# Tap rows of a deformable convolution: the multiply and the adds move from VectorE to GpSimd

## The chip, the cores and the metric

One Trainium2 chip, one core of it. The kernel is a hand-scheduled program: each engine has its own list of instructions, and semaphores hold them together. The metric is the device time of one execution in microseconds (us); of the kernel before there are three timed runs and one profiled execution. Engine names in the profile: PE is TensorE, DVE is VectorE, ACT is ScalarE, POOL is GpSimd, SP is SyncE (it only issues DMAs here).

## What is computed

A batch of 16 images of 128 channels and 56x56 pixels goes through four residual layers, each on the group-normalised image. The change sits in the second, a deformable convolution:

```python
xproj = inp @ in_w + in_b
x1 = gelu(layernorm(depthwise_conv(x)))
offset = x1 @ off_w + off_b                       # 16 groups x 9 points x (x, y)
mask = softmax((x1 @ mask_w + mask_b).reshape(N, H, W, G, P), -1)
out = _dcnv3_core(xproj, offset, mask)            # bilinear samples around each pixel, weighted by mask
out = out @ out_w + out_b
...
x = x + _L0_conv_ref(_gn(x), ...)   # whitening of 8 groups of channels
x = x + _L1_conv_ref(_gn(x), ...)   # the deformable convolution above
x = x + _L2_conv_ref(_gn(x), ...)   # attention in 7x7 windows, then between windows
x = x + _L3_conv_ref(_gn(x), ...)   # 3x3 convolution of a masked image
```

Where all offsets are below one pixel, a sample reads only the 3x3 pixels around its grid point, so the nine points together read a 5x5 neighbourhood. The bilinear weight of a point is a product of two "hats" (functions of the offset in x and in y, three values each), and the whole layer is a convolution with 25 taps whose weights differ from pixel to pixel.

## The kernel before

Samples are pipelined: one turn of the main loop (15 turns) holds the window attention of sample i beside the first steps of sample i+1 (the *windows* stretch, 32 steps `s`), and then the deformable convolution of sample i+1 beside the last two layers of sample i (the *tile* stretch). Sample 0's tile stretch stands alone ahead of the loop. The tile stretch is `sample_tiles`: 7 tiles `c` (112 partitions, each 4 pixels wide), and 5 steps `dy` in each. On every engine the program's order is what is written there; no engine may run ahead of a semaphore.

For tile `c` the steps are these.

- PE projects offsets and mask logits, ACT copies them (L1231) and makes the hats in two halves (`hats`, L1239 to L1245, at dy 1 and 2 of tile c-1). `hats` first waits for the count 3c of `k_s`, that is, until all tap rows of tile c-1 are built, since both tiles use one hat buffer.
- DVE takes the softmax of the mask: `shift_mask` (L1658, L1659) at dy 1 of tile c-1, then, after ACT's exponential, `sum_mask` and `norm_mask` (L1665 to L1671) and `rows_by_mask` (L1678), which multiplies the y hats by the mask, all at dy 3 of tile c-1.
- DVE builds the tap rows in `by_row(n, c, bb)`, bb = 0, 1, 2: one product of 1728 elements (L1690) and three additions of 576 elements into the tap weights `kw` (L1696), each waiting for the one before. bb 0 runs at dy 4 of tile c-1, bb 1 and 2 after the multiplies of dy 0 and 1 of tile c. The last addition of each raises `k_s`. For tile 0 they run in the last steps of the windows stretch and after the first multiply.
- DVE's `multiply(n, c, dy)` (L1713) makes 25 x 512 products of taps and pixels in five instructions of 2560 elements. For dy 0, 1, 2 it waits for `k_s` of bb 0, 1, 2. PE adds them up with identity matmuls (`sum_taps`, L888 and L890); the product ring holds two, so a multiply also waits for the sum two turns before.
- POOL only clears: the tap weights `kw` of each tile (L552, L556), the image, and a few paddings.

Behind each half step stands one item of the last two layers (`after_windows(i, q)`): reading the windows back from HBM, the attention between windows (q 2 to 19), the aggregation and projection (q 20 to 36; PE L978 and L988, ACT L1321, DVE L1909), the mask of the last layer (DVE L1922 to L1953) and its 63 groups of convolution matmuls (L689). SP's queue waits for `k_s` 3 of tile 0 before it loads 2 MB of weights (`load_wqk2`), and the tokens of the windows (which DVE reads at L1878, q 2) are loaded behind that in the same queue.

Below, E(c) is the moment at which the tap rows of tile c are complete (the end of the last of its three groups at L1696), and M(c) the end of `rows_by_mask` of tile c (L1678).

Of the kernel before, what the change touches and what calls it, by code (L numbers as in the profile page):

```python
# [28 lines left out]
PT = TY * TX  # L29
# [30 lines left out]
DVE_PRE, DVE_MAIN, DVE_BLK, DVE_END = 6 + 8 * DW_BLOCKS, 105, 69, 46  # L60
# [53 lines left out]
def build(nc, a):  # L114
    with ExitStack() as ctx:
# [180 lines left out]
        t_main = sem("act_own_main")  # L296
# [74 lines left out]
        def alone(eng):  # L371
            eng.sem_inc(s_passed, 1)
# [159 lines left out]
        def _(pool):  # L532
# [14 lines left out]
            def zero_taps(i, n):  # L547
                for u in range(2):
                    if i is not None:
                        pool.wait_ge(s_p.sem, s_p.at(i, PAIRS if u else PAIRS - 4))  # L550
                        alone(pool)
                    nc.gpsimd.memset(kw[u][0:PT, :], 0.0).then_inc(k_z.sem, 1)  # L552
                for c in range(2, TR):
                    pool.wait_ge(pr_s.sem, pr_s.at(n, (c - 1) * SHIFTS))
                    alone(pool)
                    nc.gpsimd.memset(kw[c % 2][0:PT, :], 0.0).then_inc(k_z.sem, 1)  # L556

# [15 lines left out]
            zero_taps(None, 0)  # L573
            with pool.Fori(0, N - 1) as i:
                zero_windows(i)
                zero_taps(i, i + 1)
# [813 lines left out]
        def _(dve):  # L1390
# [283 lines left out]
            def rows_by_mask(n, c):  # L1674
                logits, hat = logits_of(c), offsets_of(c)[1]
                dve.wait_ge(ht_s.sem, ht_s.at(n, 2 * c + 2))
                ownm.settle()
                ownm.mark(V.tensor_tensor(hat[0:PT, :, 1, :], hat[0:PT, :, 1, :],  # L1678
                                          logits.rearrange("p (a n) -> p a n", a=1).to_broadcast([PT, 3, HN]),
                                          ALU.mult))  # L1680

            def by_row(n, c, bb):

                tt, hat = terms if c else om_first, offsets_of(c)[1]
                if bb:
                    dve.wait_ge(k_s.sem, k_s.at(n, 3 * c + bb))
                else:
                    ownm.settle()
                    dve.sem_inc(rw_s.sem, 1)
                ownm.step(V.tensor_tensor(tt[0:PT, :].rearrange("p (a n) -> p a n", a=3), hat[0:PT, :, 0, :],  # L1690
                                          hat[0:PT, bb, 1:2, :].to_broadcast([PT, 3, HN]), ALU.mult))
                if bb == 0:
                    dve.wait_ge(k_z.sem, k_z.at(n, c + 1))
                for aa in range(3):
                    k5 = kw[c % 2][0:PT, :].rearrange("p (y x n) -> p x y n", y=5, x=5)[:, aa:aa + 3, bb:bb + 3, :]
                    ins = V.tensor_tensor(k5, k5, tt[0:PT, aa * HN:(aa + 1) * HN].rearrange(  # L1696
                        "p (x y n) -> p x y n", x=3, y=3), ALU.add)
                    if aa == 2:
                        ins.then_inc(k_s.sem, 1)
                    else:  # L1700
                        ownm.step(ins)
# [77 lines left out]
            def before_last(s, n):  # L1779
# [12 lines left out]
                elif s == OFF_AT + 4:  # L1792
                    rows_by_mask(n, 0)
                elif OFF_AT + 5 <= s < OFF_AT + 7:
                    by_row(n, 0, s - (OFF_AT + 5))
# [164 lines left out]
            def sample_tiles(n, i):  # L1960
                dve.wait_ge(cp_img.sem, cp_img.at(n))
                alone(dve)
                for c in range(TR):
                    ahead = c + 1 < TR
                    for dy in range(SHIFTS):
                        s = c * SHIFTS + dy
                        multiply(n, c, dy)
                        if dy == 0:
                            by_row(n, c, 1 if c else 2)
                        elif c and dy == 1:  # L1970
                            by_row(n, c, 2)
# [17 lines left out]
                        elif ahead and dy == 4:  # L1989
                            by_row(n, c + 1, 0)  # L1990
# [79 lines left out]
```

## Time and profile before

| | us |
|---|---|
| three timed runs: lowest, median, highest | 10003.76, 10026.43, 10063.13 |
| the profiled execution, its own time | 10047.3 |
| its span | 10045.3 |
| mean granted TensorE clock | 0.897 of full speed |
| busy: PE, DVE, ACT, POOL | 8162.0, 7406.0, 3949.2, 191.2 |

The profiled execution is 0.2% above the median of the timed runs. The profile gives each engine's busy time, the chain that ended last, groups of instructions by line with the idle time ahead of them and what ended it, and a timeline. A turn of the loop lasts about 588 us; the turn looked at below has its tile stretch from about 3465 to 3785 us of the span.

### The profile page before, as it was taken

What the parts mean: (1) busy time and instruction counts of PE and PEld (TensorE: products, weight loads), DVE (VectorE), ACT (ScalarE), POOL (GpSimd) and SP (SyncE); (2) the same over time, 40 slices, a digit from 0 to 9 for tenths busy, and PEclk for the clock granted to TensorE, in tenths of its full rate; (3) what the DMA queues carried; (4) which work ended last, traced back from release to release, by engine and by line L of the source; (5) the groups of instructions that cost most, each with busy time, mean ns of one, the idle gap of its engine ahead of it and who ended that gap; (6) DMA issues with size and microseconds to landing.
All of it is one profiled execution on the core that took longest, in us unless ns stands there. A gap on an engine that the chain in (4) does not pass through costs nothing.

```text
span 10045.3 us, 287502 instructions
## 1 busy us (share of the span) xinstructions
PE 8162.0 (81%) x123582; PEld 4563.3 (45%) x123582; DVE 7406.0 (74%) x8864; ACT 3949.2 (39%) x6124; POOL 191.2 (2%) x253
## 2 busy tenths in 40 slices
PE   6468888887988888798888879888887888888796
PEld 5324445353544535354453534445353444545354
DVE  2488777878777786877778687777868777786863
ACT  0034434253443435334353533434353343535332
POOL 0000000000000000000000000000000000000000
PEclk7579998998989899898999989898998989999898
DMA  4001101111110111111011111101111110111101
GB/s 113 6 13 35 49 20 46 37 38 40 42 44 22 46 31 45 41 37 48 24 46 31 45 41 33 53 22 46 31 45 42 30 54 24 46 31 45 41 25 52
DMA packets 230299, 391.48 MB, mean 39 GB/s; under 512 B 25200, under 2 KB 166480, under 8 KB 221776
## 3 DMA queue, kind: packets, MB, share of 16 engines
q1 hardware_dynamic: 229008, 372.66, 13.3%
q8 instruction: 1006, 16.48, 0.7%
q14 instruction: 285, 2.33, 0.1%
HBM read 192.47 MB, written 130.55 MB: 32 GB/s over the span
## 4 chain that ended last, share of the span: by engine, by line
PE 59%; DVE 22%; issue 11%; ACT 6%; DMA 1%; DVEq 1%; SPq 0%; POOL 0%; ACTq 0%; POOLq 0%
PE ps L888 10%; PE ps L689 7%; PE ps L753 7%; DVE arena L1713 4%; PE ps L786 4%; PE ps L988 4%; PE ps L802 4%; PE ps L761 3%; PE ps L978 3%; DVE arena L1768 3%; PE ps L710 3%; PE ps L775 2%; DVE arena L1690 2%; DVE arena L1696 2%; PE ps L922 1%
## 5 line engine op out<-in xcount | busy, mean ns | idle before, releaser
L888 PE MATMUL ps<-arena,ident 64*64 64x512 f32 x5600 | 1739.1, 677 | 745.8 <-DVE arena L1713 745.6
L890 PE MATMUL ps<-arena,ident 48*64 48x512 f32 x5600 | 1742.6, 678 | 0.0
L1713 DVE TENSOR_TENSOR arena<-arena 112x2560 f32<-112x2560 f32 x560 | 1578.2, 2819 | 100.5 <-PE ps L890 93.6
L888 PEld LDWEIGHTS ps<-arena,ident 64*64 64x64 f32 x5600 | 488.6, 148 | 1775.6 <-issue 1764.0
L753 PE MATMUL ps<-arena,wqk 128*128 128x400 f32 x2048 | 909.6, 564 | 152.6 <-DVE arena L1817 119.6
L689 PE MATMUL ps<-vp,convw 128*128 128x448 f32 x2016 | 821.3, 549 | 23.6 <-ACT vp L1310 23.6
L1696 DVE TENSOR_TENSOR arena<-arena 112x576 f32<-112x576 f32 x1008 | 764.2, 758 | 34.9
L802 PE MATMUL ps<-arena 64*64 64x33 f32 x32768 | 656.0, 229 | 127.0 <-issue 71.1
L1808 DVE TENSOR_REDUCE arena<-ps 128x16 f32<-128x800 f32 x512 | 504.9, 986 | 294.9 <-PE ps L775 290.6
L1802 DVE COPY arena<-ps 128x400 f32<-128x400 f32 x512 | 293.0, 572 | 568.2 <-PE ps L753 568.0
L1231 ACT ACTIVATE arena<-ps 112x864 f32<-112x864 f32 x224 | 199.2, 889 | 1299.8 <-PE ps L710 1295.1
L802 PEld LDWEIGHTS ps<-arena 64*64 64x64 f32 x32768 | 586.0, 144 | 229.2 <-issue 228.2
L786 PE MATMUL ps<-ident,arena 128*128 128x128 f32 x4096 | 577.4, 286 | 132.3 <-ACT arena L1109 43.8
L1690 DVE TENSOR_TENSOR arena<-arena 112x1728 f32<-112x1728 f32 x336 | 655.3, 1950 | 0.2 <-DVE arena L1678 0.2
L761 PE MATMUL ps<-wv,arena 128*64 128x256 f32 x4096 | 600.1, 417 | 37.7 <-ACT arena L1179 37.2
L753 PEld LDWEIGHTS ps<-arena,wqk 128*128 128x128 f32 x2048 | 336.1, 198 | 621.1 <-ACT arena L1166 205.9
L1173 ACT ACTIVATE arena<-arena 128x800 f32<-128x800 f32 x512 | 447.1, 873 | 367.4 <-DVE arena L1810 364.2
L689 PEld LDWEIGHTS ps<-vp,convw 128*128 128x128 f32 x2016 | 364.9, 189 | 456.2 <-issue 432.5
L775 PEld LDWEIGHTS ps<-arena 32*64 32x64 f32 x32768 | 400.0, 134 | 332.0 <-issue 324.1
L786 PEld LDWEIGHTS ps<-ident,arena 128*128 128x128 f32 x4096 | 457.1, 145 | 178.9 <-issue 128.5
L1179 ACT ACTIVATE arena<-ps 128x512 f32<-128x512 f32 x512 | 305.5, 597 | 586.7 <-PE ps L786 586.4
L1768 DVE SCALAR_TENSOR_TENSOR arena<-vp,cols,arena 128x896 f32<-128x896 f32 (+1 forms) x512 | 525.3, 1026 | 1.0
(299 smaller groups left out, 12542.5 us busy)
## 6 DMA issues: line engine op xcount, KB each, us to landing
windows_out<-arena SPq DMA_DIRECT2D x1024, 100.0 KB
arena<-windows_out SPq DMA_DIRECT2D x224, 256.0 KB, 4.2
arena<-windows_out SPq DMA_DIRECT2D x224, 192.0 KB, 3.4
arena<-in_wqk SPq DMA_DIRECT2D x16, 2048.0 KB, 8.5
arena<-in_x_t SPq DMA_DIRECT2D x16, 1568.0 KB, 10.5
arena<-in_x SPq DMA_DIRECT2D x16, 1568.0 KB, 7.3
arena<-arena SPq DMA_DIRECT2D x32, 784.0 KB
out_x<-xb SPq DMA_DIRECT2D x112, 224.0 KB, 2.0
```

The source lines that it names most:

```text
L689: mm = nc.tensor.matmul(ps[:, bank, 0:CH], weights[:, tap, :], vp[:, ROWS * k + dy:ROWS * k + dy + ROWS, dx:dx + W], start=(tap == 0), sto ...
L753: nc.tensor.matmul(ps[:, 5 - m % 2, 0:NWY * NTOK], wqk[:, m * C:(m + 1) * C], xwb[b % 2][:, :, 0:NTOK], start=True, stop=True).then_inc(qk ...
L761: mm = nc.tensor.matmul(ps[hh * SLOT:(hh + 1) * SLOT, 4, wi * 256:(wi + 1) * 256], xwb[b % 2][:, 2 * pr + wi, :], wv[:, hh * 256:(hh + 1) ...
L775: mm = nc.tensor.matmul(ps[wi * SLOT:(wi + 1) * SLOT, r, place * NTOK:(place + 1) * NTOK], qk[b % 2][32 * r:32 * r + 32, m, w:w + SLOT], q ...
L786: mm = nc.tensor.transpose(ps[:, 4 + q, k * C:(k + 1) * C], e_sb[u][:, 8 * q + 2 * k:8 * q + 2 * k + 2, :], ident)
L802: mm = nc.tensor.matmul(ps[wi * SLOT:(wi + 1) * SLOT, 6 + hh, (kk * 4 + r) * VD:(kk * 4 + r + 1) * VD], et[u][hh * SLOT:(hh + 1) * SLOT, a ...
L888: nc.tensor.matmul(ps[half, 3, :], ident[0:SLOT, 0:SLOT], prod[0:SLOT, ring(c, dy), dx, :], start=(s < 2), stop=(s >= TAPS - 2), skip_grou ...
L890: mm = nc.tensor.matmul(ps[half, 4, :], ident[SLOT:PT, SLOT:], prod[SLOT:PT, ring(c, dy), dx, :], start=(s < 2), stop=(s >= TAPS - 2), ski ...
L1690: ownm.step(V.tensor_tensor(tt[0:PT, :].rearrange("p (a n) -> p a n", a=3), hat[0:PT, :, 0, :], hat[0:PT, bb, 1:2, :].to_broadcast([PT, 3, ...
L1696: ins = V.tensor_tensor(k5, k5, tt[0:PT, aa * HN:(aa + 1) * HN].rearrange("p (x y n) -> p x y n", x=3, y=3), ALU.add)
L1713: V.tensor_tensor(prod[0:PT, ring(c, dy), :, :].rearrange("p k (n e) -> p k n e", e=CG), taps.to_broadcast([PT, SHIFTS, N64, CG]), for_tap ...
L1768: ins = V.scalar_tensor_tensor(acc, around, dww[:, tap:tap + 1], acc, ALU.mult, ALU.add)
```

## The change

GpSimd runs the three groups of one product and three additions for all seven tiles, in a function `tap_rows`, directly behind its clearing of `kw` for the same tile. DVE has `by_row` no longer; its `rows_by_mask` now raises the semaphore `rw_s` itself, and GpSimd starts on that, one step earlier than `by_row` started. Operands, sizes and order of the arithmetic are the same. DVE's multiplies, ACT's hats and SP's weight load wait for the same counts of `k_s` as before, which GpSimd now raises. GpSimd has a semaphore of its own (`pool_own_rows`) between dependent instructions.

```diff
-DVE_PRE, DVE_MAIN, DVE_BLK, DVE_END = 6 + 8 * DW_BLOCKS, 105, 69, 46
+DVE_PRE, DVE_MAIN, DVE_BLK, DVE_END = 6 + 8 * DW_BLOCKS, 35, 69, 46
+POOL_ROWS = 9 * TR
...
-            def zero_taps(i, n):
...
+            def tap_rows(n, c):
+                tt, hat = terms if c else om_first, offsets_of(c)[1]
+                pool.wait_ge(k_z.sem, k_z.at(n, c + 1))
+                alone(pool)
+                pool.wait_ge(rw_s.sem, rw_s.at(n, c + 1))
+                alone(pool)
+                for bb in range(3):
+                    if bb:
+                        pool.wait_ge(k_s.sem, k_s.at(n, 3 * c + bb))
                         alone(pool)
+                    rows.step(nc.gpsimd.tensor_tensor(
+                        tt[0:PT, :].rearrange("p (a n) -> p a n", a=3), hat[0:PT, :, 0, :],
+                        hat[0:PT, bb, 1:2, :].to_broadcast([PT, 3, HN]), ALU.mult))
                     alone(pool)
+                    for aa in range(3):
+                        k5 = kw[c % 2][0:PT, :].rearrange("p (y x n) -> p x y n", y=5, x=5)[:, aa:aa + 3, bb:bb + 3, :]
+                        ins = nc.gpsimd.tensor_tensor(k5, k5, tt[0:PT, aa * HN:(aa + 1) * HN].rearrange(
+                            "p (x y n) -> p x y n", x=3, y=3), ALU.add)
+                        if aa == 2:
+                            ins.then_inc(k_s.sem, 1)
+                        else:
+                            rows.step(ins)
+                            alone(pool)
+
+            def taps(i, n):
+                rows.turn(n, POOL_ROWS)
+                for c in range(TR):
+                    if c >= 2:
+                        pool.wait_ge(pr_s.sem, pr_s.at(n, (c - 1) * SHIFTS))
+                        alone(pool)
+                    elif i is not None:
+                        pool.wait_ge(s_p.sem, s_p.at(i, PAIRS if c else PAIRS - 4))
+                        alone(pool)
                     nc.gpsimd.memset(kw[c % 2][0:PT, :], 0.0).then_inc(k_z.sem, 1)
+                    tap_rows(n, c)
...
-                ownm.mark(V.tensor_tensor(hat[0:PT, :, 1, :], hat[0:PT, :, 1, :],
-                                          logits.rearrange("p (a n) -> p a n", a=1).to_broadcast([PT, 3, HN]),
-                                          ALU.mult))
-
-            def by_row(n, c, bb):
...
+                V.tensor_tensor(hat[0:PT, :, 1, :], hat[0:PT, :, 1, :],
+                                logits.rearrange("p (a n) -> p a n", a=1).to_broadcast([PT, 3, HN]), ALU.mult
+                                ).then_inc(rw_s.sem, 1)
...
-                        if dy == 0:
-                            by_row(n, c, 1 if c else 2)
-                        elif c and dy == 1:
-                            by_row(n, c, 2)
...
-                        elif ahead and dy == 4:
-                            by_row(n, c + 1, 0)
```

How the order of instructions moves on DVE, in the loop, from M(5) on (the mask of tile 5 is in its hats; `prod_used` is the count of summed products, `tap_rows_built` is `k_s`, `arena` is the one buffer that holds all working tiles). Before:

```order
L1678 TENSOR_TENSOR arena<-arena 112x3x576 [waits dve_own_5]
L1713 TENSOR_TENSOR arena<-arena 112x2560 [waits prod_used]
L1690 TENSOR_TENSOR arena<-arena 112x1728 [waits dve_own_5]
L1696 TENSOR_TENSOR arena<-arena 112x3x3x64 [waits taps_zeroed,dve_own_5]
...
L1713 TENSOR_TENSOR arena<-arena 112x2560 [waits tap_rows_built]
L1690 TENSOR_TENSOR arena<-arena 112x1728 [waits tap_rows_built]
L1696 TENSOR_TENSOR arena<-arena 112x3x3x64 [waits dve_own_5]
```

Now, in the same place:

```order
L1706 TENSOR_TENSOR arena<-arena 112x3x576 [waits dve_own_5]
L1720 TENSOR_TENSOR arena<-arena 112x2560 [waits prod_used]
...
L1715 REGISTER_ALU [waits prod_used]
L1720 TENSOR_TENSOR arena<-arena 112x2560 [waits tap_rows_built]
...
L1963 SCALAR_TENSOR_TENSOR xb<-ps,cols,xb 128x448 [waits conv_psum]
```

The groups of L1690 and L1696 are gone from between the multiplies, which keep their waits and their order.

On POOL, in the loop, the clearing of `kw` for tile 0 and what follows it now (`mask_in_hats` is `rw_s`, `taps_zeroed` is `k_z`):

```order
L581 MEMSET arena 112x1600 [waits s_psum]
L550 ISA
L558 TENSOR_TENSOR arena<-arena 112x1728 [waits taps_zeroed,mask_in_hats]
L112 ISA
L564 TENSOR_TENSOR arena<-arena 112x3x3x64 [waits pool_own_rows]
...
L558 TENSOR_TENSOR arena<-arena 112x1728 [waits tap_rows_built]
```

Before, two clearings stood there one behind the other and five more behind them, and nothing else. Now each clearing is followed by twelve instructions, all in one chain: three of 1728 elements and nine of 576.

## Rows read from the trace of the kernel before

**Rows 1.** The page: busy us, share of the span and instructions of each engine.

```profile
PE 8162.0 (81%) x123582; PEld 4563.3 (45%) x123582; DVE 7406.0 (74%) x8864; ACT 3949.2 (39%) x6124; POOL 191.2 (2%) x253
```

**Rows 2.** The page's groups: busy, mean ns of one, idle before it and releaser.

```profile
L888 PE MATMUL ps<-arena,ident 64*64 64x512 f32 x5600 | 1739.1, 677 | 745.8 <-DVE arena L1713 745.6
...
L1713 DVE TENSOR_TENSOR arena<-arena 112x2560 f32<-112x2560 f32 x560 | 1578.2, 2819 | 100.5 <-PE ps L890 93.6
...
L1696 DVE TENSOR_TENSOR arena<-arena 112x576 f32<-112x576 f32 x1008 | 764.2, 758 | 34.9
...
L1690 DVE TENSOR_TENSOR arena<-arena 112x1728 f32<-112x1728 f32 x336 | 655.3, 1950 | 0.2 <-DVE arena L1678 0.2
```

**Rows 3.** Waits in one tile stretch (3470 to 3780): us in total, times, longest.

```profile
PE ps L888 <- DVE arena L1713: 45.6, 8, 13.1
...
DVE xb L1909 <- PE ps L988: 23.5, 5, 6.1
```

**Rows 4.** Windows of 20 us: busy time of each engine, granted clock, DMA share.

```profile
3670.00:3690.00 20.00, 9.60 (x44) 3.23 (x45) 19.71 (x18) 7.33 (x14) 0.00 (x0) 0.66 0.00 1
...
3730.00:3750.00 20.00, 20.00 (x91) 7.99 (x91) 19.62 (x18) 1.08 (x2) 0.00 (x0) 1.00 0.06 24
```

**Rows 5.** Timeline of DVE over that stretch: start, us, line, operation, count, idle before.

```profile
3447.42 1.95 DVE L1678 TENSOR_TENSOR arena<-arena 112x1728 f32<-112x1728 f32 x1
...
3468.58 2.34 DVE L1696 TENSOR_TENSOR arena<-arena 112x576 f32<-112x576 f32 x3
...
3480.10 0.42 DVE L1878 TENSOR_REDUCE t8s<-arena 128x8 f32<-128x256 f32 x1 [6.45 <-DMA arena<-windows_out]
...
3493.36 1.96 DVE L1678 TENSOR_TENSOR arena<-arena 112x1728 f32<-112x1728 f32 x1
3495.23 2.82 DVE L1713 TENSOR_TENSOR arena<-arena 112x2560 f32<-112x2560 f32 x1
3497.97 1.95 DVE L1690 TENSOR_TENSOR arena<-arena 112x1728 f32<-112x1728 f32 x1
...
3612.47 2.82 DVE L1713 TENSOR_TENSOR arena<-arena 112x2560 f32<-112x2560 f32 x1
...
3635.28 1.96 DVE L1678 TENSOR_TENSOR arena<-arena 112x1728 f32<-112x1728 f32 x1
...
3714.14 2.82 DVE L1713 TENSOR_TENSOR arena<-arena 112x2560 f32<-112x2560 f32 x1
...
3725.18 1.96 DVE L1678 TENSOR_TENSOR arena<-arena 112x1728 f32<-112x1728 f32 x1 [0.88 <-ACT arena L1245]
...
3747.12 2.34 DVE L1696 TENSOR_TENSOR arena<-arena 112x576 f32<-112x576 f32 x3
...
3784.81 0.35 DVE L1727 SCALAR_TENSOR_TENSOR w0s<-w,r,ident 128x128 f32<-128x128 f32 x1 [4.67 <-issue]
```

**Rows 6.** POOL's groups over the whole span: busy, mean ns, idle before.

```profile
L556 POOL MEMSET arena<- 112x1600 f32 x80 | 114.5, 1431 | 3823.0 <-DVE arena L1713 3823.0
...
L562 POOL MEMSET arena<- 128x112 f32 x32 | 5.2, 192 | 1437.6 <-DVEq L1835 1437.6
...
L539 POOL MEMSET vp<- 128x3364 f32 x1 | 2.9, 2905 | 0.0
```

**Rows 7.** Timeline of POOL: a clearing in the loop.

```profile
3498.21 1.43 POOL L556 MEMSET arena<- 112x1600 f32 x1 [47.17 <-DVE arena L1713]
```

**Rows 8.** Timeline of POOL in sample 0's tile stretch: two clearings, one tile apart.

```profile
640.60 1.43 POOL L556 MEMSET arena<- 112x1600 f32 x1 [135.60 <-DVE arena L1713]
674.28 1.43 POOL L556 MEMSET arena<- 112x1600 f32 x1 [32.25 <-DVE arena L1713]
```

**Rows 9.** Timeline of DVE in sample 0: from a third multiply to M of the next tile.

```profile
795.45 5.55 DVE L1713 TENSOR_TENSOR arena<-arena 112x2560 f32<-112x2560 f32 x2
804.06 1.96 DVE L1678 TENSOR_TENSOR arena<-arena 112x1728 f32<-112x1728 f32 x1
```

**Rows 10.** ACT's groups of one tile stretch (3465 to 3785): the first of the hats' five.

```profile
L1239 ACT ACTIVATE arena<-arena 112x576 f32<-112x576 f32 x12 | 8.1, 676 | 9.9 <-DVE arena L1696 9.9
```

More of the change, by code:

```diff
@@ L295, in build @@
         d_init, d_a, d_cov, d_pow, d_pre, d_main, d_blk, d_end = (sem(f"dve_own_{k}") for k in range(8))
-        t_main = sem("act_own_main")
+        t_main, t_rows = sem("act_own_main"), sem("pool_own_rows")
         a_xt = [sig("a_xt0", 16), sig("a_xt1", 16)]
@@ L545, in _ @@
             nc.gpsimd.memset(img[0:PT, :, :, :].rearrange("p y x c -> p (y x c)"), 0.0).then_inc(s_zero, 1)
-            def zero_taps(i, n):
-                for u in range(2):
-                    if i is not None:
-                        pool.wait_ge(s_p.sem, s_p.at(i, PAIRS if u else PAIRS - 4))
+            def tap_rows(n, c):
[7 more added lines that the diff above has]
+                        pool.wait_ge(k_s.sem, k_s.at(n, 3 * c + bb))
                         alone(pool)
-                    nc.gpsimd.memset(kw[u][0:PT, :], 0.0).then_inc(k_z.sem, 1)
-                for c in range(2, TR):
-                    pool.wait_ge(pr_s.sem, pr_s.at(n, (c - 1) * SHIFTS))
+                    rows.step(nc.gpsimd.tensor_tensor(
+                        tt[0:PT, :].rearrange("p (a n) -> p a n", a=3), hat[0:PT, :, 0, :],
+                        hat[0:PT, bb, 1:2, :].to_broadcast([PT, 3, HN]), ALU.mult))
                     alone(pool)
+                    for aa in range(3):
[16 more added lines that the diff above has]
+                        alone(pool)
                     nc.gpsimd.memset(kw[c % 2][0:PT, :], 0.0).then_inc(k_z.sem, 1)
+                    tap_rows(n, c)
             def zero_windows(i):
@@ L571, in zero_windows @@
                     nc.gpsimd.memset(e_sb[u][:, :, NTOK:], 0.0).then_inc(l2_z.sem, 1)
-            zero_taps(None, 0)
+            rows = Chain(pool, t_rows)
+            taps(None, 0)
             with pool.Fori(0, N - 1) as i:
                 zero_windows(i)
-                zero_taps(i, i + 1)
+                taps(i, i + 1)
+            rows.end()
             zero_windows(N - 1)
@@ L1677, in rows_by_mask @@
                 ownm.settle()
-                ownm.mark(V.tensor_tensor(hat[0:PT, :, 1, :], hat[0:PT, :, 1, :],
-                                          logits.rearrange("p (a n) -> p a n", a=1).to_broadcast([PT, 3, HN]),
-                                          ALU.mult))
-            def by_row(n, c, bb):
[L1684 to L1701, printed above, removed]
+                V.tensor_tensor(hat[0:PT, :, 1, :], hat[0:PT, :, 1, :],
+                                logits.rearrange("p (a n) -> p a n", a=1).to_broadcast([PT, 3, HN]), ALU.mult
+                                ).then_inc(rw_s.sem, 1)
             def multiply(n, c, dy):
@@ L1793, in before_last @@
                     rows_by_mask(n, 0)
-                elif OFF_AT + 5 <= s < OFF_AT + 7:
-                    by_row(n, 0, s - (OFF_AT + 5))
             def queries_keys(i, b, m):
```

## The prediction

> **What bounds the kernel now.** I read the shares first: PE is busy 81% and DVE 74% of the span, POOL 2% [rows 1], so neither of the two is the bound all the time, and POOL is free. The groups say where PE's idle time lies: 745.6 us of it stands in front of the sums of products (L888) and was ended by DVE's multiply (L1713) [rows 2]. The waits of one tile stretch say the same for one sample, 45.6 us [rows 3]; there are 16. The windows show both kinds of place: from 3670 to 3690 DVE is busy 19.71 of 20 us, PE 9.60, and the granted clock is 0.66; from 3730 to 3750 PE is busy all 20 us at clock 1.00 and DVE 19.62 [rows 4]. So taking work from DVE can win at most about 745 us and a little clock, if the multiplies are then never late. The question is whether the tap rows, which the multiplies wait for, come in time from POOL.
>
> **What leaves DVE.** 336 products of 1950 ns and 1008 additions of 758 ns [rows 2], 655 + 764 = 1419 us, or 3 x 1.95 + 9 x 0.758 = 12.7 us for a tile. All lie between the multiplies; PE's 745.6 us of waiting is the part of them that shows. No DMA moves.
>
> **What the same rows cost on POOL.** The trace has no two-input instruction on POOL, only clearings: 112 elements in 192 ns, 1600 in 1431, 3364 in 2905 [rows 6], which is 98 ns plus 0.83 ns per element, one access each. A product or an addition makes three accesses per element, two reads and a write. If all three go at once, 1728 elements take 1.54 us and 576 take 0.58: 9.8 us for a tile. If none overlaps, 4.42 and 1.54: 27.1 us. The nearest row is one access at 0.83 ns; the two reads at least I expect one after the other, and I take 2.5 accesses, 22.8 us. Each of the twelve instructions also waits for the one before; from DVE's end (3495.23 + 2.82 = 3498.05 [rows 5]) to POOL's start on its semaphore (3498.21 [rows 7]) is 0.16 us, twelve times 1.9. That makes 24.7 us, with ends 11.7 and 29.0, against 12.7 on DVE.
>
> [...]
>
> **Do POOL and DVE hold each other up?** A clearing beside a DVE product leaves both alone: the product at 3497.97 took 1.95 us [rows 5], its mean, while POOL cleared for 1.43 [rows 7]. But a clearing reads nothing. For reads the cost lies between nothing and full exclusion. With exclusion the chain of rows of a tile must let in three multiplies (dy 4 of the tile before, dy 0, dy 1), which become ready exactly when the chain starts or hands over, since they wait for the same M(c) and the same `k_s`; with a mask subtraction that is 3 x 2.82 + 0.7 = 9.2 us. I take the upper end as the likelier, so a chain of R = 24.7 + 9.2 = 33.9 us; ends 11.7 and 38.2.
>
> That choice leans on a page: the Trainium skill (SBUF — State Buffer, Who interferes with whom) says that a VectorE instruction with two SBUF inputs and a GpSimd instruction that reads SBUF exclude each other for the whole instruction, and it speaks against this change. By it R is some 34 us, without it 25.
>
> **The path that decides.** E(c), the end of the rows, releases both DVE's third multiply and ACT's hats for tile c+1; those lead to M(c+1), and M(c+1) starts POOL's next rows. So E to E is now a closed loop, [E(c) to M(c+1)] + R, however idle DVE is. Before, the six loops from E(0) = 3470.9 to E(6) = 3749.5 took 278.6 us [rows 5], 46.4 each.
>
> - E to M. For tile 0 it runs over SP: E(0) lets the weight load and then the token load go, the tokens are there at 3480.10, and M(1) ends at 3495.3: 24.4 us [rows 5], unchanged. For the others I take the third multiply to the end of L1678: from 24.8 us (3612.47 to 3637.2) down to 13.0 (3714.14 to 3727.1) [rows 5], the six together 111.3. In the middle three DVE waits for PE, most of it in front of L1909 (23.5 us in the stretch [rows 3]); PE can now catch up while POOL works, and I take 13.3 off: 98. ACT's hats hardly shorten this: two halves of five instructions of about 0.68 us [rows 10], an exponential and a copy between them, make some 8 to 9 us after E, then 2.0 for L1678.
> - R six times: 6 x 33.9 = 203.4, plus 4 in tile 4, where DVE also makes the mask of the last layer from SBUF.
> - Together 305.4 against 278.6: **+26.8 us** a sample.
> - Start. M(0) is at 3447.42 + 1.95 = 3449.4 [rows 5]; POOL's rows of tile 0 take 24.7 beside DVE work that reads mostly PSUM, and two multiplies 5.6: E(0) at 3479.7 instead of 3470.9, **+8.8**. DVE's windows stretch is shorter by two groups, but the third multiply waits for E(0) all the same.
> - End. From E(6) to the next turn (3784.81) are 35.3 us [rows 5], PE working off convolutions; a PE that had waited is not behind there. I take 25: **-10**.
>
> That is +25.6 us a turn, 384 us over 15. Sample 0 has no other work beside its tiles: 674.28 - 640.60 = 33.7 us a tile [rows 8], of which 10.6 from third multiply to M (795.45 to 806.0 [rows 9]). It becomes 10.6 + 33.9 = 44.5: six times 10.8, and 9 for the start, 74. Sum: 384 + 74 = **+458 us**. Against the profiled execution's 10047 that is 10505; that execution is 21 us above the median of the timed runs, so for a median I say **10485 us**. The loop breaks even at R near 29.6 us.
>
> Costs at nothing: the clearing of `kw` (1.43 us [rows 7]) falls between E(c) and M(c+1), where POOL has nothing else; if M came within 1.4 us of E it would add to R. The 2 MB weights start 9 us later with E(0), but so do their users.
>
> **Rivals.**
>
> *No exclusion: faster.* If POOL's reads and DVE's leave each other alone, R = 24.7. The loop gives 98 + 148 = 246; while the windows are aggregated (tiles 2 and 3) PE sets the pace and gives some 10 of it back: -22. Start +3.2, end -5: -24 a turn, -360; sample 0: 6 x (35.3 - 33.7) + 3 = +13. Time 10026 - 347 = 9680. For it: the clearings show no clash. It decides from R below 29.6. 0.22.
>
> *POOL near its clearing pace: faster.* With R about 12 the rows are in time everywhere, and most of the 745.6 us goes: 9300 to 9400. Against it: three accesses per element. 0.05.
>
> *A wash.* R at 28 to 31, or E to M shorter than I take it: within 50 us of now. 0.11.
>
> *Slower, and by more.* Three accesses in full and exclusion, R = 38.2: 4.3 x 6 x 16 = 413 us more, 10900. PE, idle more often, would also drop to the lower clock (the stretch at 0.66 [rows 4]) and stretch E to M. This lies on my forecast's side. 0.15, beside 0.47 for the forecast itself, whose own range is 10250 to 10750.
>
> That the rows would not move is excluded by the order of instructions.
>
> **How the numbers follow.** A measurement of this kernel tells about 0.5%, 50 us, from no change. Faster by more: 0.22 + 0.05, and a little of the wash, 0.28. Same: 0.10. Slower: 0.62. The range takes in the forecast, the wash, the no-exclusion case at 9680 and the slow end at 10900; it leaves out the fastest case and what lies beyond 10950.
>
> **What would show.** DVE's busy time falls by about 1420 us, POOL's rises from 191 to 2.5 to 3.8 ms. The ends of two chains of rows of one sample lie about 50 us apart on average instead of 46. DVE's waits in front of the multiply name POOL, PE's 745 us in front of L888 grow, and the granted clock falls. Exclusion shows as multiplies above 2.82 us or starting late, and as POOL products longer beside them. The prediction is wrong if POOL's 1728 take under 2.5 us, if the multiplies keep 2.82 us and POOL's chain 25 us, or if E to M shrinks below 12 us on average.

## The result, and the profile after

The changed kernel takes **10694.7 us** (median of four runs, 10686.6 to 10718.5), the kernel before, run beside it, 10038.7 (10003.8 to 10063.1). The ratio is 1.066, 95% interval 1.0622 to 1.0698: slower by 656 us. The profiled spans are 10716.8 and 10045.3 us, 671.5 apart. The forecast, 10485, had the sign; the time lies in the range, and in the forecast's own (10250 to 10750), 210 us above the forecast. Those 210 us have a place.

The page of the changed kernel: the span, busy time, and of the chain that ended last the shares by engine and by line.

```profile
span 10716.8 us, 288541 instructions
PE 8297.7 (77%) x123582; PEld 4617.4 (43%) x123582; DVE 6374.7 (59%) x7520; ACT 3948.9 (37%) x6124; POOL 3748.9 (35%) x1597
PE 36%; POOL 27%; DVE 20%; issue 10%; ACT 4%; DMA 1%; POOLq 0%; DVEq 0%; SPq 0%; ACTq 0%
POOL arena L558 16%; POOL arena L564 11%; PE ps L781 6%; PE ps L916 3%; PE ps L814 3%; PE ps L830 3%; PE ps L1016 3%; DVE arena L1720 3%; DVE arena L1775 3%; PE ps L789 3%; PE ps L1006 2%; PE ps L803 2%; DVE arena L1706 2%; PE ps L717 1%; DVE arena L1813 1%
```

POOL went from 191 us busy [rows 1] to 3749, and its rows alone are 27% of the chain that sets the end, though POOL is idle two thirds of the time. DVE lost 1031 us and not the 1419 that left it: its remaining work is not all at its old length. The mean granted clock fell from 0.897 to 0.883.

The groups of the same page. Lines moved: the multiply is now L1720 (L1713 before), the sum of products L916 (L888), POOL's product L558, its additions L564, its clearing of `kw` L581, `rows_by_mask` L1706.

```profile
L916 PE MATMUL ps<-arena,ident 64*64 64x512 f32 x5600 | 1877.3, 723 | 1314.9 <-DVE arena L1720 1314.6
L558 POOL TENSOR_TENSOR arena<-arena 112x1728 f32<-112x1728 f32 x336 | 2077.3, 6182 | 2152.7 <-DVE arena L1706 2112.7
L1720 DVE TENSOR_TENSOR arena<-arena 112x2560 f32<-112x2560 f32 x560 | 1622.2, 2898 | 1776.2 <-POOL arena L564 1752.5
L564 POOL TENSOR_TENSOR arena<-arena 112x576 f32<-112x576 f32 x1008 | 1485.9, 1474 | 180.2 <-POOL arena L564 120.2
```

PE's wait for the multiply ahead of the sums grew from 745.6 us [rows 2] to 1314.6. It still reads "<-DVE", but DVE itself now waits 1752.5 us for POOL ahead of the multiply, and POOL 2112.7 us for `rows_by_mask`: the closed loop of the prediction, DVE to POOL to DVE, shown as two waits that name each other.

**What a tile of rows looks like.** POOL's timeline (start, duration; in brackets idle time and releaser), the chain of tile 0 in one turn and the first product of tile 1:

```profile
3689.03 3.86 POOL L558 TENSOR_TENSOR arena<-arena 112x1728 f32<-112x1728 f32 x1 [25.48 <-DVE arena L1706]
3693.06 1.41 POOL L564 TENSOR_TENSOR arena<-arena 112x576 f32<-112x576 f32 x1 [0.18 <-POOL arena L558]
3694.66 1.40 POOL L564 TENSOR_TENSOR arena<-arena 112x576 f32<-112x576 f32 x1 [0.18 <-POOL arena L564]
...
3697.81 3.84 POOL L558 TENSOR_TENSOR arena<-arena 112x1728 f32<-112x1728 f32 x1 [0.18 <-POOL arena L564]
3701.83 3.76 POOL L564 TENSOR_TENSOR arena<-arena 112x576 f32<-112x576 f32 x1 [0.18 <-POOL arena L558]
...
3708.92 6.38 POOL L558 TENSOR_TENSOR arena<-arena 112x1728 f32<-112x1728 f32 x1 [0.18 <-POOL arena L564]
...
3744.68 6.25 POOL L558 TENSOR_TENSOR arena<-arena 112x1728 f32<-112x1728 f32 x1 [23.29 <-DVE arena L1706]
```

And DVE's in the same stretch:

```profile
3697.95 6.37 DVE L1720 TENSOR_TENSOR arena<-arena 112x2560 f32<-112x2560 f32 x1
3708.77 2.83 DVE L1720 TENSOR_TENSOR arena<-arena 112x2560 f32<-112x2560 f32 x1 [4.45 <-POOL arena L564]
3742.54 1.96 DVE L1706 TENSOR_TENSOR arena<-arena 112x1728 f32<-112x1728 f32 x1
3744.41 2.82 DVE L1720 TENSOR_TENSOR arena<-arena 112x2560 f32<-112x2560 f32 x1
```

Alone, a product takes POOL 3.84 to 3.86 us and an addition 1.40. Where a multiply began first (3708.77, 3744.41), POOL's product takes 6.25 to 6.38 and ends 6.5 us after the multiply began: the multiply's 2.82 and then its own 3.84 would be 6.66. Of the 336 products of the span 305 began under a running multiply, and each of them took over 5.5 us. Where POOL began first (3697.81), its product keeps 3.84 and DVE's multiply takes 6.37, and the addition that comes due meanwhile (3701.83) takes 3.76. One runs, the other stands, whole instructions at a time. The Trainium skill (SBUF — State Buffer, Who interferes with whom) says just this of a VectorE instruction with two SBUF inputs and a GpSimd instruction that reads SBUF; the trace agrees. The wait of each POOL instruction for the one before is 0.18 us.

The twelve instructions alone, without the handovers, are 3 x 3.86 + 9 x 1.40 = 24.2 us a tile. The Trainium skill (GPSIMD Engine Reference, Elementwise: side-by-side cycle accounting) gives 4497 ns for a two-input float32 addition of 2048 elements on GpSimd; scaled by the number of elements alone, that is an estimate of 22.8 us, and the trace is 6% above it.

**One turn, by its E and M** (from POOL's and DVE's timelines; M and E as defined before the prediction, R = E - M is the time from the mask product to the last of the tile's rows, and the last column is M less the E of the tile before; `w0s` is the first DVE instruction of a turn):

| tile | M | E | R = E - M | E to M |
|---|---|---|---|---|
| 0 | 3688.85 | 3720.0 | 31.2 | |
| 1 | 3744.5 | 3778.5 | 34.0 | 24.5 |
| 2 | 3790.5 | 3825.3 | 34.8 | 12.0 |
| 3 | 3843.5 | 3877.6 | 34.1 | 18.2 |
| 4 | 3900.3 | 3936.4 | 36.1 | 22.6 |
| 5 | 3958.7 | 3992.8 | 34.1 | 22.4 |
| 6 | 4003.95 | 4037.7 | 33.8 | 11.2 |

Six loops: R 207, E to M 111, together 317.7 us against 278.6 before: +39.1. E(6) to the next `w0s` (4062.53) is 24.8 against 35.3. From the turn's own `w0s` to E(0) it is 289.3 in this turn against 273.1, but that stretch varies from turn to turn by more than 10 us, so the averages over all turns say more: +9.1 ahead of E(0), +40.9 for the six loops (319.3 against 278.4) and -10.8 behind E(6). A turn is 626.4 us on average against 587.3, 39.1 longer. Fourteen such turns are 547.5 us; with 81.0 more up to the first turn (sample 0) and 43.0 in the last turn, which runs to the end of the span, they are the 671.5 of the spans.

### The profile page after: what moved, and what is told of

Read it like the earlier page. It is cut to its first block, busy times and chain, and to the rows that moved or that the text cites. A ratio compares the mean times of both kernels' runs of the same rounds, so it can differ in the third digit from the quotient of the medians.

```text
span 10716.8 us, 288541 instructions
## 1 busy us (share of the span) xinstructions
PE 8297.7 (77%) x123582; PEld 4617.4 (43%) x123582; DVE 6374.7 (59%) x7520; ACT 3948.9 (37%) x6124; POOL 3748.9 (35%) x1597
## 4 chain that ended last, share of the span: by engine, by line
PE 36%; POOL 27%; DVE 20%; issue 10%; ACT 4%; DMA 1%; POOLq 0%; DVEq 0%; SPq 0%; ACTq 0%
POOL arena L558 16%; POOL arena L564 11%; PE ps L781 6%; PE ps L916 3%; PE ps L814 3%; PE ps L830 3%; PE ps L1016 3%; DVE arena L1720 3%; DVE arena L1775 3%; PE ps L789 3%; PE ps L1006 2%; PE ps L803 2%; DVE arena L1706 2%; PE ps L717 1%; DVE arena L1813 1%
## 5 line engine op out<-in xcount | busy, mean ns | idle before, releaser
L916 PE MATMUL ps<-arena,ident 64*64 64x512 f32 x5600 | 1877.3, 723 | 1314.9 <-DVE arena L1720 1314.6
L558 POOL TENSOR_TENSOR arena<-arena 112x1728 f32<-112x1728 f32 x336 | 2077.3, 6182 | 2152.7 <-DVE arena L1706 2112.7
L1720 DVE TENSOR_TENSOR arena<-arena 112x2560 f32<-112x2560 f32 x560 | 1622.2, 2898 | 1776.2 <-POOL arena L564 1752.5
L918 PE MATMUL ps<-arena,ident 48*64 48x512 f32 x5600 | 1885.8, 724 | 0.0
L916 PEld LDWEIGHTS ps<-arena,ident 64*64 64x64 f32 x5600 | 534.1, 156 | 2405.5 <-issue 2398.6
L564 POOL TENSOR_TENSOR arena<-arena 112x576 f32<-112x576 f32 x1008 | 1485.9, 1474 | 180.2 <-POOL arena L564 120.2
L581 POOL MEMSET arena<- 112x1600 f32 x112 | 160.4, 1432 | 3341.0 <-PE ps L803 3341.0
L814 PE MATMUL ps<-ident,arena 128*128 128x128 f32 x4096 | 575.2, 285 | 138.2 <-ACT arena L1137 43.6
```

The costliest lines, as they stand in the source:

```text
L558: rows.step(nc.gpsimd.tensor_tensor(tt[0:PT, :].rearrange("p (a n) -> p a n", a=3), hat[0:PT, :, 0, :], hat[0:PT, bb, 1:2, :].to_broadcast ...
L564: ins = nc.gpsimd.tensor_tensor(k5, k5, tt[0:PT, aa * HN:(aa + 1) * HN].rearrange("p (x y n) -> p x y n", x=3, y=3), ALU.add)
L814: mm = nc.tensor.transpose(ps[:, 4 + q, k * C:(k + 1) * C], e_sb[u][:, 8 * q + 2 * k:8 * q + 2 * k + 2, :], ident)
L916: nc.tensor.matmul(ps[half, 3, :], ident[0:SLOT, 0:SLOT], prod[0:SLOT, ring(c, dy), dx, :], start=(s < 2), stop=(s >= TAPS - 2), skip_grou ...
L918: mm = nc.tensor.matmul(ps[half, 4, :], ident[SLOT:PT, SLOT:], prod[SLOT:PT, ring(c, dy), dx, :], start=(s < 2), stop=(s >= TAPS - 2), ski ...
L1720: V.tensor_tensor(prod[0:PT, ring(c, dy), :, :].rearrange("p k (n e) -> p k n e", e=CG), taps.to_broadcast([PT, SHIFTS, N64, CG]), for_tap ...
```

## The experiments

Ten kernels, each one edit on the changed kernel unless said otherwise. Theory A: POOL's chain R, a third of it exclusion, in a closed loop with E to M. Rivals: any DVE work slows POOL; exclusion costs nothing, POOL is just slow; the late tokens; E to M could be cut.

### The multiply with one input

```diff
-                V.tensor_tensor(prod[0:PT, ring(c, dy), :, :].rearrange("p k (n e) -> p k n e", e=CG),
-                                taps.to_broadcast([PT, SHIFTS, N64, CG]), for_taps, ALU.mult).then_inc(pr_s.sem, 1)
+                V.tensor_scalar(prod[0:PT, ring(c, dy), :, :].rearrange("p k (n e) -> p k n e", e=CG),
+                                for_taps, 0.04, None, ALU.mult).then_inc(pr_s.sem, 1)
```

> Changed kernel, but the multiply of taps and pixels is one scaling of the pixels by a constant: same shape and place, one input from SBUF instead of two (this leaves out the weighting of the pixels by the taps). Theory 1 (the multiplies, with two SBUF inputs, and GpSimd's reads exclude each other): GpSimd's product falls from 6.2 us on average to 3.9, a tile's rows from about 34 us to 26.3 (three times 3.86 + 0.18, nine times 1.40 + 0.18), and with six loops in each of 15 turns the kernel takes 9900 to 10050 us. Rival A (any VectorE instruction beside GpSimd slows it): product stays near 6.2 us and the time within 0.5% of 10695. Rival B (GpSimd's own arithmetic is the whole cost and exclusion costs the path nothing): the product shortens or not, the time stays above 10550.

Measured: 10181.1 us, ratio 1.0146 (1.0119 to 1.0173). The page's groups:

```profile
L1720 DVE TENSOR_SCALAR arena<-arena 112x2560 f32<-112x2560 f32 x560 | 1575.4, 2814 | 1267.0 <-POOL arena L564 1235.2 <-PE ps L918 31.7
L558 POOL TENSOR_TENSOR arena<-arena 112x1728 f32<-112x1728 f32 x336 | 1294.9, 3854 | 2287.2 <-DVE arena L1706 2247.3 <-POOL arena L564 40.0
```

The kernel leaves out the weighting by the taps. The multiply is as long as ever (2.81 us) and as often beside POOL's products (319 of 336; 320 in the changed kernel), which now keep 3854 ns on average where they took 6182, none above 3.89 us. So it is not the multiply's activity that stops POOL but its second SBUF input. The exclusion of the multiplies is worth 514 of the 656 us. But the time missed my range by 130 us: the loops of the profiled turn sum to 281.7, where six times 26.3 and the 98 us that I had forecast for E to M would be 256.

### Its control: the kernel before with the same multiply

> The kernel before, with the multiply as a one-input operation (pixels times a constant): like the run one_input, it leaves out the weighting by taps. It is the control of that run: there the changed kernel with this multiply took 1.015 of the kernel before. If the form of the multiply does nothing by itself, this one takes what the kernel before takes, 10000 to 10060 us, and what the run one_input gained is exclusion alone. If the one-input multiply (of the same 2.81 us) shortens something else, it is below 9950, and the part of the changed kernel's loss that exclusion makes is smaller than I said by that much.

Measured: 10033.4, ratio 1.0013 (0.9997 to 1.0028). As expected, the edit does nothing by itself; what it gave the changed kernel is the end of the exclusion.

### One addition in place of three

```diff
-POOL_ROWS = 9 * TR
+POOL_ROWS = 3 * TR
...
-                    for aa in range(3):
+                    for aa in (2,):
```

> The changed kernel with one of the three additions of each group (the last) instead of three; it leaves out the other two, so six of nine additions of a tile. The multiplies keep both inputs and exclude POOL. POOL's chain of rows loses 6 x (1.40 + 0.18) = 9.5 us a tile, R falls from 34 to about 24.5. If the loop E to M plus R is what decides, E(0) to E(6) falls by less than six times 9.5, because E to M takes slack up as in the run one_input, which had R near 26.5 and 10181 us: 10050 to 10200. If it is the holding up of the multiplies themselves that costs (they still clash three times a tile), the time stays above 10400.

Measured: 9999.4 us, ratio 0.9965 (0.9943 to 0.9987): 50 us below my range. The kernel leaves out six of the nine additions of a tile. The multiplies still exclude POOL: the products average 5951 ns and 282 of 336 began under a running multiply:

```profile
3475.49 6.24 POOL L558 TENSOR_TENSOR arena<-arena 112x1728 f32<-112x1728 f32 x1 [23.13 <-DVE arena L1706]
3481.91 1.40 POOL L564 TENSOR_TENSOR arena<-arena 112x576 f32<-112x576 f32 x1 [0.18 <-POOL arena L558]
3483.49 6.38 POOL L558 TENSOR_TENSOR arena<-arena 112x1728 f32<-112x1728 f32 x1 [0.18 <-POOL arena L564]
```

So the clashes do not keep the kernel slow by themselves; what counts is what they add to R. With this run, and two that follow below, the loop can be read at six values of R. Sums of the six loops of a turn, averages over the 15 turns:

| kernel | R, six | E to M, six | loops | median us |
|---|---|---|---|---|
| changed | 206.7 | 112.6 | 319.3 | 10695 |
| first group on DVE | 178.6 | 125.6 | 304.3 | 10526 |
| one input | 162.7 | 121.6 | 284.3 | 10181 |
| only the third group on POOL | 161.7 | 122.4 | 284.1 | 10178 |
| one addition | 148.7 | 128.3 | 277.0 | 9999 |
| before (rows on DVE) | 140.2 | 138.2 | 278.4 | 10039 |

The two kernels with R near 162 reach it by different edits, one with exclusion and one without, and take the same time. As R shrinks, E to M mostly grows. With one input and with one addition most of that growth (8.7 of 9.0 us, 10.5 of 15.7) is at one place, E(3) to M(4), which takes 23.9 us in the changed kernel, 32.6 and 34.4 in these two, and 33.1 before. There DVE has little to do but wait. DVE's timeline with one addition, between E(3) at 3581.85 and M(4) at 3615.0:

```profile
3586.99 0.68 DVE L1914 SCALAR_TENSOR_TENSOR xb<-ps,cols,xb 128x448 f32<-128x448 f32 x1 [10.44 <-PE ps L1016]
...
3590.22 2.82 DVE L1720 TENSOR_TENSOR arena<-arena 112x2560 f32<-112x2560 f32 x1
3597.53 0.68 DVE L1914 SCALAR_TENSOR_TENSOR xb<-ps,cols,xb 128x448 f32<-128x448 f32 x1 [4.50 <-PE ps L1016]
...
3607.85 0.68 DVE L1914 SCALAR_TENSOR_TENSOR xb<-ps,cols,xb 128x448 f32<-128x448 f32 x1 [6.14 <-PE ps L1016]
...
3613.03 1.96 DVE L1706 TENSOR_TENSOR arena<-arena 112x1728 f32<-112x1728 f32 x1
```

Three additions of the aggregated windows (L1914; L1909 before) stand in DVE's order ahead of M(4), each waiting for PE's L1016. With the changed kernel's late E(3) only two come behind it, the first with a wait of 2.31 us:

```profile
3877.66 2.83 DVE L1720 TENSOR_TENSOR arena<-arena 112x2560 f32<-112x2560 f32 x1 [1.30 <-POOL arena L564]
3882.80 0.68 DVE L1914 SCALAR_TENSOR_TENSOR xb<-ps,cols,xb 128x448 f32<-128x448 f32 x1 [2.31 <-PE ps L1016]
3893.12 0.68 DVE L1914 SCALAR_TENSOR_TENSOR xb<-ps,cols,xb 128x448 f32<-128x448 f32 x1 [6.14 <-PE ps L1016]
```

PE's aggregation sets a pace that a faster chain of rows runs into. On a straight line between the ratios with R sums of 149 and 163 (0.9965 and 1.0146), 1 is passed near 152. That is an estimate of R = 25.3 us a tile for the break even, where I had 29.6; it is rough, since the two kernels differ in tile 0 as well (M(0) to E(0) 21.6 and 26.3).

### Only some of the rows on POOL

Group bb 0 of each tile back on DVE, directly behind `rows_by_mask`; POOL makes bb 1 and 2:

```diff
+                            by_row(n, c + 1, 0)
...
-                for bb in range(3):
+                for bb in (1, 2):
```

> Changed kernel, but the first of the three groups of rows of each tile is made by VectorE again, directly behind the mask product; GpSimd makes the second and third. Theory 1: a tile's rows take 4.4 us on VectorE, 2 x 8.8 on GpSimd and 8.4 of three multiplies that it lets in, about 30.5 us instead of 34.4, and the start of the tile stretch comes 4 us earlier: 28 us a turn, time 10200 to 10300 us. Rival B (only GpSimd's busy time counts): it falls by a third, 11 us a tile, time below 9900. Rival D (VectorE's load is the bound again): above 10600.

Measured: 10526.1, ratio 1.0479 (1.0449 to 1.051), 230 us above my range. POOL's products still average 5955 ns, and the additions rose from 1474 to 1934: with the first group gone, the clashes come down on what is left. But R was not what I had wrong: it is 29.2 to 30.9 us a tile against the 30.5 I expected, 28 us a turn less than in the changed kernel. Of these 28, E to M took back 13.0 (125.6 against 112.6), and the stretch from E(6) to the next M(0) 7.6 (283.7 against 276.1), so a turn is only 8.6 us shorter. Why that last stretch is longer no run took apart.

Groups bb 0 and 1 on DVE where they stood before, only bb 2 on POOL:

> VectorE makes the first and second group of rows of every tile at their old places, GpSimd only the third. Theory 1: the third group takes 8.8 us on GpSimd and 2.8 us of the multiply that it lets in, 11.3 in place of 4.3, on the path E to M to E in six of seven tiles, while VectorE is free for 1.9 us of mask work and more meanwhile; in tile 4, where VectorE has some 13 us of the last layer's mask at that place, it gains instead. Some 20 us a turn, time 10250 to 10400 us: slower than before although VectorE loses 470 us of work. Rival B (VectorE's load is what counts): 10026 less up to 300, below 9950.

Measured: 10177.6, ratio 1.0135 (1.0111 to 1.0158), 72 us below my range. POOL's 112 products average 5024 ns. Even one group of three is a loss.

All three groups of tile 0 on DVE, the other tiles on POOL:

> Changed kernel, but the rows of tile 0 alone are made by VectorE, where they stood before; GpSimd makes those of tiles 1 to 6. Theory 1: M(0) to E(0) goes back from 31 us to 21.5, the six loops behind it stay as they are, so a turn is 9 to 10 us shorter and the time 10530 to 10560 us. Rival (the rows of tile 0 are hidden in the windows stretch, or cost VectorE's windows work as much as they bring): within 30 us of 10695.

Measured: 10558.8, ratio 1.0512 (1.0488 to 1.0536), 136 us below the changed kernel, as expected: from M(0) to E(0) it is 31.2 us against 21.5, and 9.7 x 15 turns = 146.

### The mask earlier

ACT's exponential ahead of the hats, both hats behind E(c), DVE's softmax ahead of the multiply of dy 2, and multiply dy 3 and `rows_by_mask` right behind it:

```diff
+                        if ahead and dy == 2:
+                            sum_mask(n, c + 1)
+                            norm_mask(n, c + 1)
+                        if not (dy == 3 and ahead):
+                            multiply(n, c, dy)
+                        if dy == 2 and ahead:
+                            multiply(n, c, 3)
+                            rows_by_mask(n, c + 1)
```

> Changed kernel with the steps between the end of a tile's rows E(c) and the next mask product M(c+1) cut short: ACT's exponential goes ahead of the hats, both halves of the hats follow E(c) at once, VectorE sums and normalises the mask before it waits for E(c), and the multiply of dy 3 and the mask product come right behind the multiply of dy 2. Theory 1 (the path is the loop E to M to E, so E to M counts in full however idle VectorE is): E to M falls from 17 us (tiles 2 to 6) to 9.5, about 35 us a turn, and the time to 10150 to 10250 us; GpSimd's rows stay at 34 us. Rival B (GpSimd's rows alone set the pace, and what stands between them is hidden): no change, above 10600. Rival C (PE, late and at the lower clock, sets the pace): less than half of it, above 10450.

Measured: 10814.2, ratio 1.077 (1.074 to 1.0801): slower than the change itself, 560 us above my range. In some of the six loops E to M did fall, into tile 3 from 18.2 to 11.7 us and into tile 6 from 11.2 to 9.0; but into tile 4 it rose from 22.6 to 38.4 and into tile 5 from 22.4 to 26.8. Over the 15 turns E to M averages 120.0 us for the six against 112.6, and R 204.8 against 206.7. Ahead of M(4) DVE stands, in its order, behind both kinds of late neighbour:

```profile
3873.77 4.01 DVE L1721 TENSOR_TENSOR arena<-arena 112x2560 f32<-112x2560 f32 x1
3888.49 0.68 DVE L1915 SCALAR_TENSOR_TENSOR xb<-ps,cols,xb 128x448 f32<-128x448 f32 x1 [10.71 <-PE ps L1016]
...
3894.95 1.13 DVE L1694 TENSOR_REDUCE softmax_sum<-arena 112x64 f32<-112x576 f32 x1 [3.16 <-ACT arena L1278]
...
3911.54 1.96 DVE L1707 TENSOR_TENSOR arena<-arena 112x1728 f32<-112x1728 f32 x1 [8.61 <-ACT arena L1273]
```

10.7 us for PE's aggregation, then 3.2 for ACT's exponential and 8.6 for its hats, which wait in turn behind ACT's copies of what PE aggregates. My reading is that moving the mask forward in the order moved the last layers' items back, which PE's aggregation then waits for; this run shows the waits, and no run took the two moves apart.

### The tokens ahead of the weights

```diff
                 sp.wait_ge(k_s.sem, k_s.at(n, 3))
+                for u in range(2):
+                    sp.wait_ge(wf_out[u].sem, wf_out[u].at(i))
+                for hh in range(2):
+                    sp.dma_start(tok[hh * SLOT:(hh + 1) * SLOT, :], ...)
                 sp.dma_start(wqk2, a["wqk2"]).then_inc(wq_in.sem, 16)
```

> Changed kernel, with the tokens of the windows loaded ahead of the 2 MB of weights in SP's queue; both still wait for the rows of tile 0. Theory 1 (the first loop of a turn, E(0) to M(1), is held by that load): VectorE finds the tokens about 4 us after E(0) instead of 9.3, the turn is 4 to 6 us shorter and the time 60 to 90 us less, 10605 to 10635. Rival (the wait is for the windows' own stores, or the path runs elsewhere): within 20 us of 10695.

Measured: 10617.2, ratio 1.0577 (1.055 to 1.0604), 78 us below the changed kernel. DVE's wait for the tokens, over the whole span, in the changed kernel, then with the tokens first:

```profile
DVE t8s L1883 <- DMA arena<-windows_out: 269.1, 16, 17.7
```

```profile
DVE t8s L1883 <- DMA arena<-windows_out: 176.7, 16, 11.5
```

92 us of wait less, 78 us of time. In the profiled turn E(0) to M(1), the one E to M that runs over SP, falls from 24.5 to 18.2. In the kernel before the wait is 103.9 us with the same 24.4 from E(0) to M(1): the wait alone had grown, because DVE has less to do ahead of it.

### The kernel before with the tokens first

All rows on DVE, in their old places, and only the order of SP's queue changed:

> All rows on VectorE as before the change, with the tokens of the windows loaded ahead of the 2 MB of weights in SP's queue. The load order is worth about 5 us a turn in the changed kernel; before the change VectorE stands 6.45 us at that wait with nothing else to do. Expected: 9940 to 9970 us, 0.6 to 0.9% faster than before. Rival (PE, not VectorE, is late there): within 20 us of before.

Measured: **9956.5 us, ratio 0.9919 (0.9901 to 0.9938)**: 0.8% faster than the kernel before, a small gain but clear of the noise, and as expected. DVE's wait for the tokens, before and in this run:

```profile
DVE t8s L1878 <- DMA arena<-windows_out: 103.9, 16, 10.6
```

```profile
DVE t8s L1909 <- DMA arena<-windows_out: 9.2, 15, 5.5
```

E(0) to M(1) falls from 24.2 to 18.2 us on average over the turns. The edit gives the kernel before what it gave the changed one (82 us here, 78 there).

### And one group a sample on POOL

As that, with only the last group of tile 4 on POOL, where DVE also makes the last layer's mask:

> As the kernel with all rows on VectorE and the tokens first, but the third group of rows of tile 4 alone is GpSimd's. There VectorE has the last layer's mask, some 13 us, between the multiplies of dy 1 and 2, which covers the 11.3 us of GpSimd. Theory 1: VectorE's 4.3 us come off the path, 65 us over 15 turns, time 9870 to 9910 us. Rival (exclusion takes it back: the mask's sums with two inputs wait for GpSimd, up to 3.9 us each): no faster than its sibling, 9940 to 9970.

Measured: 9940.6, ratio 0.9908 (0.9885 to 0.9931; runs from 9915 to 9982). The 16 us below the run before are within both intervals; the 46 to 87 I expected are not there. It is the rival's range (9940 to 9970), and its cause is in the profile: POOL's 48 additions average 2899 ns and not 1400.

## Why the prediction was right, and where it was off

- **What leaves DVE**: right, 1419 us; but I expected the busy time to fall by as much, and it fell by 1031. Added up group by group, what stayed on DVE is 356 us longer (388 in the page's busy time, which counts overlaps of neighbours once), and only 44 of them are the multiplies (1622.2 against 1578.2, mean 2898 ns); the others are small instructions beside POOL, below.
- **POOL's own pace**: predicted 2.5 accesses, 24.7 us with the handovers. Measured 3 x 3.86 + 9 x 1.40 + 12 x 0.18 = 26.3. 1.6 us more, inside the ends of 11.7 and 29.0 that POOL's clearings [rows 6] gave.
- **Exclusion**: the choice of the upper end was right. 9.2 us a tile were predicted; measured R is 33.8 to 34.8 in the plain tiles against 26.3 alone, 7.5 to 8.5. This error and the one in POOL's pace cancel, and that is luck: six times R is 207, predicted 207.4 with the 4 of tile 4 (there 36.1). Exclusion of the multiplies costs 514 us, by the run with one input and its control.
- **E to M**: this is the term that was mis-sized. Predicted 98 us for the six, measured 110.9 in the profiled turn and 112.6 on average: 14.6 us a turn, 219 us over 15, which is all of the 210 us that the forecast was short (the rest nearly cancels). It failed in two places, read here in the profiled turn. I counted from the third multiply, as if it came right behind E(c); before the change it came late in tile 4, E(4) at 3664.0 and the multiply at 3676.65, with the mask of the last layer between them. That mask work is still there, and now inside E to M: 22.4 us where I had counted 13.9, +8.5. And I took 13.3 us off for PE that catches up; the other four gained only 3.8, 1.2, 2.2 and 1.8, 9.0 in all. In the loops where the windows are aggregated DVE still stands at L1914 for PE, as the lines above show for E(3) to M(4).
- **Start and end**: +8.8 predicted ahead of E(0), +9.1 measured on average (M(0) to E(0) is 31.2 against 21.5). Behind E(6) I took 25 us, and it is 24.8. Both right.
- **A turn**: +39.1 against +25.6. **Sample 0**: 44.8 us a tile from E to E (predicted 44.5), but E(0) comes 16.2 us later and not 9; in all +81.0 us against 74.
- **The rivals.** "No exclusion: faster, 9680" falls twice: there is exclusion, and without it the kernel takes 10181, still slower than before. Its mistake is the forecast's own, and POOL's pace beside it. It put the six loops at 256 us (148 of R, and 98 of E to M with 10 given back); the run with one input has 163 and 119, 281.7. The condition it named, R below 29.6, is refuted: R was 27 there and the kernel still slower than before. What the runs suggest is near 25. POOL at 26.3 alone is past it even in peace. "Near its clearing pace" falls with 3.86 us. "Slower, and by more" had 10900 by R = 38.2; the time went half of the way from the forecast to it, not by R but by E to M; the clock fell by 0.014 only.
- **The sign** hung less on exclusion than I wrote. It takes the loss from 1.5% to 6.6%.

Open: whether a second hat buffer, which would let ACT's hats start before E(c), would open the loop. It wasn't tried; the arena has no room for it.

## What to carry to other kernels

Before work moves to an idle engine, look for the loop it closes: the old place may have been late for reasons of its own, and these return as soon as the new chain is shorter. A chain on POOL beside DVE work with two SBUF inputs costs its own length plus, nearly, every such DVE instruction that falls due inside it; here almost every product of the chain began beside one (320 of 336), since the multiplies were released by the same steps. An engine's idle time in an average (POOL 2%, DVE 74%) tells neither; one turn, laid out as ends of the links of the loop, tells both. And an edit that was made to explain a loss is worth trying on the kernel before by itself: here the order of two loads in one queue gave 0.8%.

## What the runs showed of the hardware

DVE instructions with two SBUF inputs are held for as long as POOL's product or addition lasts, however short they are themselves. DVE's timeline of the changed kernel, in the last layer's mask, while POOL ran its last product and additions of tile 4 (3922.90 to 3936.3):

```profile
3925.49 1.79 DVE L1929 TENSOR_TENSOR arena<-vp 128x1568 f32<-128x1568 f32 x1
3927.32 4.49 DVE L1930 TENSOR_TENSOR arena<-arena 128x784 f32<-128x784 f32 x1
3931.84 1.65 DVE L1931 TENSOR_TENSOR arena<-arena 128x392 f32<-128x392 f32 x1
3933.52 0.89 DVE L1932 TENSOR_REDUCE arena<-arena 128x56 f32<-128x392 f32 x1
...
3935.61 2.11 DVE L1940 TENSOR_SCALAR sm<-sm 128x2 f32<-128x2 f32 x1
```

POOL's product in that stretch, which waited for the multiply at 3922.75 and for L1929 behind it:

```profile
3922.90 8.07 POOL L558 TENSOR_TENSOR arena<-arena 112x1728 f32<-112x1728 f32 x1 [0.18 <-POOL arena L564]
```

And POOL's clearing at the end of it, behind its last addition (3934.93 to 3936.33):

```profile
3936.27 1.43 POOL L581 MEMSET arena<- 112x1600 f32 x1
```

In the kernel before, the same DVE instructions:

```profile
3663.87 1.79 DVE L1924 TENSOR_TENSOR arena<-vp 128x1568 f32<-128x1568 f32 x1
3665.69 0.98 DVE L1925 TENSOR_TENSOR arena<-arena 128x784 f32<-128x784 f32 x1
3666.70 0.57 DVE L1926 TENSOR_TENSOR arena<-arena 128x392 f32<-128x392 f32 x1
3667.30 0.88 DVE L1927 TENSOR_REDUCE arena<-arena 128x56 f32<-128x392 f32 x1
...
3669.34 0.23 DVE L1935 TENSOR_SCALAR sm<-sm 128x2 f32<-128x2 f32 x1
```

The addition of 784 elements takes 4.49 us and not 0.98, that of 392 takes 1.65 and not 0.57; the reduction, with one input, keeps its 0.89.

L1940 works on two numbers a partition, with its scalar read from SBUF, and takes 2.11 us for 0.23. It is a case of its own. It began under POOL's addition but did not end with it: it ended at 3937.72, 0.02 us after POOL's clearing (3936.27 + 1.43 = 3937.70), an instruction that reads nothing, and so it did in all 15 turns of the loop. A clearing beside a DVE product left both alone in the kernel before ([rows 5], [rows 7]), and the prediction took clearings for harmless; this instruction a clearing does hold. So it is not only reads on both sides that exclude each other. The TENSOR_SCALAR multiply of L1720 in the run with one input, whose scalar is a constant, was not held by POOL's products. What sets L1940 apart no run here shows.

Over the whole span the largest group of held instructions is the mask's subtraction, in the changed kernel and before:

```profile
L1687 DVE TENSOR_TENSOR arena<-arena,softmax_max 112x576 f32<-112x576 f32 x112 | 208.4, 1861 | 3.8
```

```profile
L1659 DVE TENSOR_TENSOR arena<-arena,softmax_max 112x576 f32<-112x576 f32 x112 | 84.9, 758 | 3.9
```

That is 123.5 of the 356 us; L1930 has 52.7, a 128x1 instruction of the normalisation's statistics (L1571, 48 times, now 1277 ns on average) 50.8, L1907 40.2, L1940 28.1. I had priced the multiplies and one subtraction a tile, and took such work to be too small to matter. Which part of these 312 us (356 less the multiplies' 44) lies on the path that sets the end, no run shows.
